# Graph stack, layer 2: the maximum of the squared norms travels over the partitions by two DMAs through memory

## The chip, the cores and the metric

One Trainium2 chip, one core of it. The metric is device time in microseconds (us) of one execution; three runs of the kernel before are given, and their median counts. The engines are called PE (TensorE), DVE (VectorE), ACT (ScalarE), POOL (GpSimd) and SP (SyncE, which here only issues DMAs).

## What is computed

Four graph layers in a row on x of 16 graphs x 1024 nodes x 64 features, with one adjacency matrix of 1024 x 1024. Each layer takes `h = max(layernorm(x), 0)` and adds its result to x. Layers 0 and 3 are graph attention with additive scores, layer 1 is an attention by channel, layer 2 is the one of this change:

```
def _gat_layer(h, mask, b):
    scores = einsum('...nd,...md->...nm', h, h)
    scores = where(mask, scores, NEG)
    attn = softmax(scores, axis=-1)
    return einsum('...nm,...md->...nd', attn, h) + b

h = einsum('bnc,hdc->bhnd', x, Wh)                 # 4 heads of 64
out_h = _gat_layer(h, mask, bh)
z = leaky_relu(concatenated heads, 0.2)
h2 = einsum('bnk,dk->bnd', z, Wo)
out2 = _gat_layer(h2, mask, bo)                    # the output attention
out = layernorm(leaky_relu(out2, 0.2)) * gamma + beta
```

The softmax needs an upper bound of the scores so that the exponential stays finite. A score is a dot product of two rows of h, so no score is above the largest squared norm of a row. That maximum over the 1024 nodes is what the change is about.

## The kernel before, in words

Layer 2 is a list of 80 **units** (`UNITS`): for each of 16 graphs the heads 0 and 1, then the output attention of the graph before, then heads 2 and 3; the last unit (`LAST`) is the output attention of the last graph and runs inside layer 3. Nodes lie on 128 partitions in 8 tiles, so a unit has 8 **weights** (jt = 0 to 7). For each weight PE makes scores of 128 x 1024 into one of two PSUM tiles (`dots`, L1795), ACT takes the exponential into a ring in SBUF (`weights`, L1042), DVE multiplies by the mask (`masked_weights`, L1388), and PE multiplies it with the values and sums (`dot_sums`, `weigh`, L1614). PE runs its sums three weights behind its scores (`LAG`).

Every engine's order is written out by hand. Beside the weights of unit n the kernel prepares unit n+1 (`nxt`), at fixed weights of each engine's `dot_unit`:

- PE: values (jt 0, `values`, L1838) and their transposes (jt 2, `features`, L1847) into a PSUM pair `AX`, whose two banks have their users in an order that `AX_AT` lists; a user waits until the one before has given the bank back (`ax_free`). Twice in a graph it also turns finished heads (`turn_heads`, L1815), which takes both banks: at jt 5 of head 3 and at jt 6 of the next graph's head 0.
- ACT: copies the values and squares them (`sq`, L1063), copies the transposes as fp16 (`hi`, L1076).
- DVE: row sums of the squares and their maximum per partition (`norms`, jt 1: L1413, `norm2_max` L1415); the fp16 remainder of the transposes (`feature_rest`, jt 3: `lo`, L1405), which gives bank 1 back; the end of the unit before (`epilogue`, jt 3: `recip` L1396, `leaky` L1397, shown as score); the bound (`bias`, jt 4: `norm2_all` L1421, `dot_bias` L1423). Buffer digits are left out in the profile, so `norm2_max` reads norm_max.
- PE, for the bound: `spread_bound` (jt 3) multiplies the column `norm2_max`, broadcast, with the identity, so that every partition gets all 128 maxima as a row in bank 0 of `AX` (`spread`, L1604, the line is shared with the two attention layers). DVE's `bias` reads that row and gives bank 0 back.
- SP: for each unit four DMAs move `hi` into `FA`, and when `lo` is made four more move `lo` (L507, L508, L513, L514). The first `dots` of the next unit wait until all eight have landed. Each wait holds back every later DMA of SP.

ACT's first exponential of a unit waits for its `dot_bias`; POOL divides a finished unit (`divide`, L794) after DVE's epilogue.

Of the kernel before, what the change touches and what calls it, by code (L numbers as in the profile page):

```python
# [11 lines left out]
P = 128  # L12
D = 64
ALU = mybir.AluOpType
ACT = mybir.ActivationFunctionType
F32 = mybir.dt.float32
# [14 lines left out]
def gnn_stack(nc, x, adj, w_gat0, w_gat0_t, a_gat0, w0, b0, wa, ba, wh_t, bh, wo_t, bo, gamma, beta,  # L31
# [11 lines left out]
    with ExitStack() as ctx:  # L43
# [85 lines left out]
        norm2_max = sb("norm2_max", [P, 1])  # L129
        norm2_all = sb("norm2_all", [P, 1])  # L130
        dot_bias = sb("dot_bias", [P, 3])

# [140 lines left out]
        sq_made = sem("sq_made")  # L273
        bound_dve = sem("bound_dve")
        z_epi = sem("z_epi")
        on_dve = sem("on_dve")
# [130 lines left out]

        def place_bound(u):

            place(("N", u["n"]), 0)  # L410

        def place_pair(name, b, q):
# [7 lines left out]
        place_features(UNITS[0])  # L420
        place_bound(UNITS[0])
        for u in UNITS[:-1]:
            if after(u):
                place_values(after(u))
                place_features(after(u))
                place_bound(after(u))
            if is_head(u, 0) and u["b"] > 0:
                place_pair("Z", u["b"] - 1, 2)
            if is_head(u, 2) and u["b"] + 1 < B:
                place_norm(2, u["b"] + 1)  # L430
            if u is BEFORE:
                place_norm(3, 0)
                place_peak(3, 0)
                place_norm(3, 1)
            if is_head(u, 3):
                place_pair("Z", u["b"], 0)
# [10 lines left out]
        place_features(LAST)  # L447
        place_bound(LAST)
        place_peak(3, FIRST + 1)
# [39 lines left out]
        def _(sp):  # L489
# [10 lines left out]
            for u in UNITS:  # L500
                par = buf_of(u)
                moved = features_in[par]
                sp.wait_ge(hi_made, u["n"] + 1)
                for half in range(2):
                    cols_of = slice(half * HALF, (half + 1) * HALF)
                    own = slice(half * D, (half + 1) * D)
                    sp.dma_start(FA[0:D, par, 0, cols_of], hi[own, par, :]).then_inc(moved, 16)  # L507
                    sp.dma_start(FA[D:P, par, 1, cols_of], hi[own, par, :]).then_inc(moved, 16)  # L508
                sp.wait_ge(lo_made, u["n"] + 1)
                for half in range(2):  # L510
                    cols_of = slice(half * HALF, (half + 1) * HALF)
                    own = slice(half * D, (half + 1) * D)
                    sp.dma_start(FA[D:P, par, 0, cols_of], lo[own, par, :]).then_inc(moved, 16)  # L513
                    sp.dma_start(FA[0:D, par, 1, cols_of], lo[own, par, :]).then_inc(moved, 16)  # L514
# [642 lines left out]
        def _(dve):  # L1157
# [259 lines left out]
            def bias(u):  # L1417
                buf = buf_of(u)
                k, at = AX_AT["N", u["n"]]
                dve.wait_ge(ax_full[k], at + 1)  # L1420
                dve.tensor_reduce(norm2_all[:, :], AX[k][:, 0:P], AX_X, ALU.max).then_inc(ax_free[k], 1)  # L1421
                dve.wait_ge(ax_free[k], at + 1)
                dve.tensor_scalar(dot_bias[:, buf:buf + 1], norm2_all[:, :], -1.0, DOT_LIFT, ALU.mult, ALU.add)\  # L1423
                    .then_inc(bound_dve, 1)
# [18 lines left out]
            def dot_unit(u, jt):  # L1443
# [3 lines left out]
                if jt == 1 and nxt:  # L1447
                    norms(nxt)
                if jt == 3 and nxt:
                    feature_rest(nxt)  # L1450
                if jt == 3 and 0 < u["n"] < LAST["n"]:
                    epilogue(UNITS[u["n"] - 1])
                if jt == 4 and nxt:
                    bias(nxt)
# [28 lines left out]
            def last_layer():  # L1483
# [13 lines left out]
                for jt in range(T):  # L1497
                    gat_weights(3, 1, jt)
                    if jt == 0:
                        node_peak(3, 2)  # L1500
                        stat_mean(3, B - 2)
                    if jt == 2:
                        gat_reciprocal(3, 0)
                    if jt == 3:
                        norms(LAST)
                    if jt == 5:
                        feature_rest(LAST)
                    if jt == 6:
                        bias(LAST)
                    if jt == 7:  # L1510
                        stat_var(3, B - 2)

                for jt in range(T):
# [40 lines left out]
        def _(pe):  # L1554
# [159 lines left out]
            def last_layer():  # L1714
# [12 lines left out]
                for jt in range(T):  # L1727
# [5 lines left out]
                    if jt == 2:  # L1733
                        features(LAST)
                    if jt == 4:
                        spread_bound(LAST)

# [111 lines left out]

            def spread_bound(u):  # L1850

                pe.wait_ge(bound_dve, 3 * u["n"] + 2)
                spread(take_bank(AX_AT["N", u["n"]]), norm2_max[:, 0:1])

            def turn_next(b):
                turn_norm(2, b)

            def dot_unit(u, jt):
# [3 lines left out]
                if jt == LAG - 1 and after(u):  # L1862
                    features(after(u))
                if jt == 3 and after(u):
                    spread_bound(after(u))
                if jt == 6 and is_head(u, 0) and b > 0:
# [12 lines left out]
            def dot_layer():  # L1879
                spread_bound(UNITS[0])  # L1880
                end = T * LAST["n"]
# [56 lines left out]
```

## Time and profile before

| | us |
|---|---|
| median of 3 runs (2016.5 to 2019.79) | 2018.07 |
| span of the profiled execution, first to last instruction | 2015.0 |
| PE busy in the span | 1913.5 (95%) |
| DVE busy | 1684.4 (84%) |
| ACT busy | 1234.0 (61%) |
| POOL busy | 1065.5 (53%) |

The profiled execution's own time is its span with what lies around it. The page gives the span; against the lowest of the runs 1.5 us lie around it, against the median 3.1 us. TensorE's granted clock is 0.987 of full speed over the span. Layer 2 takes the time from about 440 us to about 1780 us.

### The profile page before, as it was taken

Reading aid. Unit: us, or ns where it says so; the run is one execution under the profiler, and the core shown is the slowest. Engines: PE = TensorE matmul, PEld = TensorE weight load, DVE = VectorE, ACT = ScalarE, POOL = GpSimd, SP = SyncE. Lnnn points to the kernel's source line nnn. Section 1 sums busy time; section 2 is a strip of 40 time slices with the busy share of each in tenths; the row PEclk is TensorE's granted clock in tenths of the full one; section 3 lists DMA queues with packets and bytes.
Section 4 is the critical chain, followed back from the end, with each engine's and each line's share of the span. In section 5 each row is a group of like instructions: output and inputs, shape, how many; then the busy total and the mean of one; then the engine's idle time right before and its main releaser. Section 6 shows DMA issues by size and latency. Waiting matters only on the chain.

```text
span 2015.0 us, 95064 instructions
## 1 busy us (share of the span) xinstructions
PE 1913.5 (95%) x43624; PEld 1569.7 (78%) x43624; DVE 1684.4 (84%) x2007; ACT 1234.0 (61%) x1842; POOL 1065.5 (53%) x754
## 2 busy tenths in 40 slices
PE   7888789989999999999999999999999999989998
PEld 6777689977777777777777777777777777767887
DVE  6988988868788888888888888888888888867998
ACT  5776655426666666666666666666666666654342
POOL 6787888622344545545454544545545445354653
PEclk8999999989999999999999999999999999999999
DMA  7000000001111111111111111111111111101111
GB/s 181 4 4 3 3 2 2 2 14 38 32 33 34 33 34 34 35 34 35 34 35 34 33 34 34 29 36 30 33 34 35 34 35 34 34 14 24 25 25 35
DMA packets 88255, 61.24 MB, mean 30 GB/s; under 512 B 45616, under 2 KB 86832, under 8 KB 87856
## 3 DMA queue, kind: packets, MB, share of 16 engines
q1 hardware_dynamic: 85632, 54.57, 11.1%
q8 instruction: 343, 5.62, 1.2%
q10 hardware_dynamic: 2224, 0.59, 0.1%
q14 instruction: 56, 0.46, 0.1%
HBM read 8.98 MB, written 4.19 MB: 7 GB/s over the span
## 4 chain that ended last, share of the span: by engine, by line
PE 70%; DVE 13%; POOL 9%; ACT 4%; issue 3%; DMA 0%; SPq 0%; ACTq 0%; POOLq 0%; DVEq 0%
PE ACC L1614 30%; PE S L1795 24%; PE S L1774 5%; DVE ring L1388 4%; PE AX L1838 3%; PE AX L1847 2%; DVE ring L1241 2%; PE AX L1815 2%; POOL sp_log L778 1%; POOL ln_sq L781 1%; DVE ch_rden L1373 1%; POOL below L626 1%; PE AX L1594 1%; POOL st_rstd L553 1%; ACT ring L1042 1%
## 5 line engine op out<-in xcount | busy, mean ns | idle before, releaser
L1614 PEld LDWEIGHTS ACC<-V,ring 128*64 128x64 f32 x28672 | 957.4, 138 | 184.6 <-issue 38.8
L1388 DVE TENSOR_TENSOR ring<-ring,mask_self_t 128x1024 f32<-128x1024 f32 x640 | 893.2, 1405 | 192.3 <-ACT ring L1042 187.9
L1614 PE MATMUL ACC<-V,ring 128*64 128x65 f32 x28672 | 976.7, 223 | 31.7 <-DVE ring L1241 13.7
L1042 ACT ACTIVATE ring<-S,dot_bias 128x1024 f32<-128x1024 f32 x640 | 713.8, 1116 | 410.3 <-PE S L1795 373.1
L1795 PE MATMUL S<-FA 128*64 128x512 f16 x5120 | 666.1, 382 | 1.4 <-DMA FA<-lo 1.4
L1795 PEld LDWEIGHTS S<-FA 128*64 128x64 f16 x5120 | 253.5, 110 | 161.1 <-ACT ring L1042 15.8
L1241 DVE SCALAR_TENSOR_TENSOR ring<-S,pair_q,mask_t 128x1024 f32<-128x1024 f32 x256 | 315.1, 1272 | 15.3 <-DVE f_max L1253 4.7
L794 POOL TENSOR_TENSOR EV_both<-score,recip 128x512 f32<-128x512 f32 x64 | 124.4, 1943 | 316.5 <-DVE score L1397 316.4
L1774 PE MATMUL S<-parts,mask_t 128*128 128x128 bf16 x3072 | 176.0, 220 | 12.9 <-DVE X L1377 11.6
L1774 PEld LDWEIGHTS S<-parts,mask_t 128*128 128x128 bf16 x3072 | 174.3, 99 | 14.6 <-issue 14.6
L787 POOL TENSOR_TENSOR V<-v_pairs,bh_bc 128x512 f32<-128x512 f32 x64 | 96.6, 1509 | 119.2 <-ACT v_pairs L1062 119.2
L866 ACT ACTIVATE accs<-ACC 128x520 f32<-128x520 f32 x112 | 66.8, 597 | 90.3 <-PE ACC L1614 90.3
L593 POOL TENSOR_TENSOR ln_rstd<-ln_ve,neg_half 128x8 f32<-128x8 f32 x32 | 74.0, 2311 | 79.2 <-DVE ln_ve L1232 66.8
L794 POOL TENSOR_TENSOR relu_z<-score,recip 128x512 f32<-128x512 f32 x16 | 30.4, 1900 | 108.8 <-DVE score L1397 108.8
L1062 ACT ACTIVATE v_pairs<-AX 128x512 f32<-128x512 f32 x80 | 47.8, 598 | 56.1 <-PE AX L1838 56.1
L553 POOL TENSOR_TENSOR st_rstd<-st_ve,neg_half 128x8 f32<-128x8 f32 (+1 forms) x31 | 66.1, 2133 | 22.3 <-ACT st_ve L899 17.5
L642 POOL TENSOR_TENSOR V<-V 128x512 f32<-128x512 f32 x32 | 33.3, 1041 | 56.7 <-ACT V L923 56.6
L778 POOL TENSOR_TENSOR sp_log<-relu_z,on_mean 128x512 f32<-128x512 f32 x16 | 30.4, 1901 | 54.2 <-DVE on_mean L1431 54.2
L1413 DVE TENSOR_REDUCE norm<-sq 128x8 f32<-128x512 f32 x80 | 54.1, 677 | 5.2 <-ACT sq L1063 5.2
L1373 DVE RECIPROCAL ch_rden<-S 128x512 f32<-128x512 f32 x16 | 53.6, 3348 | 5.7 <-PE S L1774 5.4
L1405 DVE TENSOR_TENSOR lo<-AX,hi 128x512 f16<-128x512 f32 x80 | 54.6, 682 | 1.1 <-ACT hi L1076 1.1
L1847 PE MATMUL AX<-ident,v_pairs 128*128 128x128 f32 x320 | 53.3, 290 | 1.5 <-ACTq L1068 1.5
(131 smaller groups left out, 2017.6 us busy)
## 6 DMA issues: line engine op xcount, KB each, us to landing
FA<-hi SPq DMA_DIRECT2D x320, 64.0 KB, 2.0
FA<-lo SPq DMA_DIRECT2D x320, 64.0 KB, 2.0
X<-in_x SPq DMA_DIRECT2D x16, 256.0 KB, 5.0
ring<-in_adj SPq DMA_DIRECT2D x8, 512.0 KB, 8.1
out_x<-X SPq DMA_DIRECT2D x16, 256.0 KB, 2.6
wh<-in_wh_t ACTq DMA_DIRECT2D x2, 64.0 KB, 6.5
bh_bc<-in_bh ACTq DMA_DIRECT2D x1, 128.0 KB, 9.5
w_gat<-in_w_gat ACTq DMA_DIRECT2D x4, 16.0 KB, 3.9
```

What stands on the lines that cost most here:

```text
L553: pool.tensor_tensor(stat_of(st_rstd, layer, b, count), stat_of(st_ve, layer, b, count), neg_half[:, 0:count * T], ALU.pow).then_inc(st_rs ...
L593: pool.tensor_tensor(ln_rstd[:, :], ln_ve[:, :], neg_half[:, 0:T], ALU.pow).then_inc(ln_pool, 1)
L787: pool.tensor_tensor(halves_of(V[:, u["n"] % 3, :, 1:D + 1]), v_pairs, halves_of(chans(bias)), ALU.add)\
L794: pool.tensor_tensor(dst, tiles(leaky[:, :]), cols(recip[:, :]), ALU.mult).then_inc(z_epi, 1)
L1042: act.activation(ring[:, jt, :], S[jt % 2][:, :], ACT.Exp, bias=dot_bias[:, n % 2:n % 2 + 1])\
L1241: dve.scalar_tensor_tensor(out=ring[:, jt, :], in0=S[par][:, :], scalar=pair_q[:, par, jt:jt + 1], in1=mask_t[:, jt, :], op0=ALU.max, op1= ...
L1373: dve.reciprocal(tiles(ch_rden[:, :]), sums[:, :, D:2 * D]).then_inc(ch_recip, 1)
L1388: dve.tensor_tensor(ring[:, jt, :], ring[:, jt, :], mask_self_t[:, jt, :], ALU.mult)\
L1614: last = pe.matmul(acc_of(t)[rows, :], ring[:, jt, t * P + c * CUT:t * P + (c + 1) * CUT], values, start=(jt == 0 and t % 4 == 0), stop=(j ...
L1774: last = pe.matmul(S[par][:, t * P:(t + 1) * P], mask_t[:, j, t * P:(t + 1) * P], parts[:, par, part, j, :], start=(j == 0 and part == 0), ...
L1795: last = pe.matmul(S[jt % 2][rows, cut], FA[:, buf, 0, jt * P + c * CUT:jt * P + (c + 1) * CUT], FA[:, buf, i, cut], start=(i == 0), stop= ...
L1847: last = pe.transpose(AX[k][:, q * P:(q + 1) * P], v_by_pair[:, q * P:(q + 1) * P], ident[:, :])
```

## The change

`norm2_max`, one number per partition, is written by a DMA to a row of 128 floats in memory, and a second DMA reads that row back into every partition (`norm2_bc`, 128 x 128). SP issues the first ahead of the four `hi` moves, the second between `hi` and `lo`. DVE's `bias` reads `norm2_bc` instead of PSUM, at jt 6 instead of 4 (for the last unit after jt 7 of its unit of layer 3 instead of after 6). The epilogue of the unit before goes to jt 2 instead of 3, ahead of the third weight's `lo`. PE's `spread_bound` and its place among the users of bank 0 are gone. In the changed file the lines after the declarations lie a few numbers further (L1388 is L1390, L1795 is L1793).

```diff
+        norm2_row = nc.dram_tensor("norm2_row", [2, P], F32, kind="Internal").ap()
+        norm2_bc = sb("norm2_bc", [P, P])
...
-        def place_bound(u):
-            place(("N", u["n"]), 0)
...
@@ SP
             for u in UNITS:
                 par = buf_of(u)
                 moved = features_in[par]
+                sp.wait_ge(bound_dve, 3 * u["n"] + 2)
+                sp.dma_start(norm2_row[par], norm2_max[:, 0:1]).then_inc(bound_out, 16)
                 sp.wait_ge(hi_made, u["n"] + 1)
                 for half in range(2):
...
+                sp.wait_ge(bound_out, 16 * (u["n"] + 1))
+                sp.dma_start(norm2_bc[:, :], norm2_row[par].partition_broadcast(P)).then_inc(bound_in, 16)
                 sp.wait_ge(lo_made, u["n"] + 1)
@@ DVE
             def bias(u):
                 buf = buf_of(u)
-                k, at = AX_AT["N", u["n"]]
-                dve.wait_ge(ax_full[k], at + 1)
-                dve.tensor_reduce(norm2_all[:, :], AX[k][:, 0:P], AX_X, ALU.max).then_inc(ax_free[k], 1)
-                dve.wait_ge(ax_free[k], at + 1)
+                dve.wait_ge(bound_in, 16 * (u["n"] + 1))
+                dve.tensor_reduce(norm2_all[:, :], norm2_bc[:, :], AX_X, ALU.max).then_inc(bound_maxed, 1)
+                dve.wait_ge(bound_maxed, u["n"] + 1)
                 dve.tensor_scalar(dot_bias[:, buf:buf + 1], norm2_all[:, :], -1.0, DOT_LIFT, ALU.mult, ALU.add)\
                     .then_inc(bound_dve, 1)
...
+                if jt == 2 and 0 < u["n"] < LAST["n"]:
+                    epilogue(UNITS[u["n"] - 1])
                 if jt == 3 and nxt:
                     feature_rest(nxt)
-                if jt == 3 and 0 < u["n"] < LAST["n"]:
-                    epilogue(UNITS[u["n"] - 1])
-                if jt == 4 and nxt:
+                if jt == 6 and nxt:
                     bias(nxt)
...
-                    if jt == 6:
-                        bias(LAST)
                     if jt == 7:
                         stat_var(3, B - 2)
+                        bias(LAST)
@@ PE
-            def spread_bound(u):
-                pe.wait_ge(bound_dve, 3 * u["n"] + 2)
-                spread(take_bank(AX_AT["N", u["n"]]), norm2_max[:, 0:1])
...
-                if jt == 3 and after(u):
-                    spread_bound(after(u))
```

PE in head 3 of a graph, before, from the transposes of the next unit to the turning of heads 0 and 1 (EV_both is where finished heads lie):

```order
L1847 MATMUL AX<-ident,v_pairs 128x128 x4
L1795 MATMUL S<-FA 64x512 x8
L1614 MATMUL ACC<-V,ring 64x65 x16
L1604 MATMUL AX<-ident,norm_max 64x128 x2
L1795 MATMUL S<-FA 64x512 x8
L1614 MATMUL ACC<-V,ring 64x65 x16
L1795 MATMUL S<-FA 64x512 x8
L1614 MATMUL ACC<-V,ring 64x65 x16
L1815 MATMUL AX<-ident,EV_both 128x128 x8
```

PE at the same place, now:

```order
L1845 MATMUL AX<-ident,v_pairs 128x128 x4
L1793 MATMUL S<-FA 64x512 x8
L1614 MATMUL ACC<-V,ring 64x65 x16
L1793 MATMUL S<-FA 64x512 x8
L1614 MATMUL ACC<-V,ring 64x65 x16
L1793 MATMUL S<-FA 64x512 x8
L1614 MATMUL ACC<-V,ring 64x65 x16
L1813 MATMUL AX<-ident,EV_both 128x128 x8
```

The two matmuls of the spread are gone, and with them a user of bank 0 between the values and the turned heads.

DVE in the same head 3, before, from the norms to the bound, with each row's waits:

```order
L1413 TENSOR_REDUCE norm<-sq 128x8 [waits sq_made]
L1415 TENSOR_REDUCE norm_max<-norm 128x1 [waits bound_dve]
L1388 TENSOR_TENSOR ring<-ring,mask_self_t 128x1024 [waits exp_done] x2
L1405 TENSOR_TENSOR lo<-AX,hi 128x512 [waits hi_made]
L1396 RECIPROCAL recip<-accs 128x8 [waits lo_made,acc_copied]
L1397 SCALAR_TENSOR_TENSOR score<-accs 128x512
L1388 TENSOR_TENSOR ring<-ring,mask_self_t 128x1024 [waits exp_done]
L1421 TENSOR_REDUCE norm_all<-AX 128x1 [waits ax_full0]
L1423 TENSOR_SCALAR dot_bias<-norm_all 128x1 [waits ax_free0]
```

DVE at the same place, now:

```order
L1415 TENSOR_REDUCE norm<-sq 128x8 [waits sq_made]
L1417 TENSOR_REDUCE norm_max<-norm 128x1 [waits bound_dve]
L1390 TENSOR_TENSOR ring<-ring,mask_self_t 128x1024 [waits exp_done]
L1398 RECIPROCAL recip<-accs 128x8 [waits acc_copied]
L1399 SCALAR_TENSOR_TENSOR score<-accs 128x512
L1390 TENSOR_TENSOR ring<-ring,mask_self_t 128x1024 [waits exp_done]
L1407 TENSOR_TENSOR lo<-AX,hi 128x512 [waits hi_made]
L1390 TENSOR_TENSOR ring<-ring,mask_self_t 128x1024 [waits lo_made,exp_done]
L1390 TENSOR_TENSOR ring<-ring,mask_self_t 128x1024 [waits exp_done] x2
L1422 TENSOR_REDUCE norm_all<-norm_bc 128x1 [waits bound_in]
L1424 TENSOR_SCALAR dot_bias<-norm_all 128x1 [waits bound_maxed]
```

The epilogue stands one weight sooner and now ahead of `lo`; the bound stands two weights later and waits for a DMA.

SP, the DMAs of one unit, now (before, there are the four of `hi` and the four of `lo` alone):

```order
L502 DMA norm_row<-norm_max 128x1 [waits bound_dve]
L507 DMA FA<-hi 64x512 [waits hi_made]
L508 DMA FA<-hi 64x512
L510 DMA norm_bc<-norm_row 128x128 [waits bound_out]
L515 DMA FA<-lo 64x512 [waits lo_made]
L516 DMA FA<-lo 64x512
```

The rows of `hi` and of `lo` each stand there twice, one pair after the other. One DMA is added ahead of `hi`, and one, with a wait for the first, ahead of `lo`.

## Rows read from the trace of the kernel before

**Rows 1.** The page, busy time and the chain that ended last, by engine.

```profile
PE 1913.5 (95%) x43624; PEld 1569.7 (78%) x43624; DVE 1684.4 (84%) x2007; ACT 1234.0 (61%) x1842; POOL 1065.5 (53%) x754
...
PE 70%; DVE 13%; POOL 9%; ACT 4%; issue 3%; DMA 0%; SPq 0%; ACTq 0%; POOLq 0%; DVEq 0%
```

**Rows 2.** Busy time by stretch: 15 graphs of layer 2, with clock and DMA share.

```profile
480.00:1760.00 1280.00, 1260.35 (x27648) 994.00 (x27646) 1078.90 (x1303) 856.93 (x972) 602.71 (x331) 1.00 0.14 34
```

**Rows 3.** Waits of PE: total us, times, longest us.

```profile
PE AX L1815 <- DVE norm_all L1421: 19.6, 15, 1.7
...
PE S L1795 <- DMA FA<-lo: 1.4, 1, 1.4
```

**Rows 4.** The chain in order of time, 1014 to 1044 us: start, us, what.

```profile
1016.10 0.61 DVE lo L1405
...
1016.85 0.20 DVE recip L1396
1017.05 0.56 DVE score L1397
...
1018.75 0.21 DVE norm_all L1421
...
1019.09 1.07 PE AX L1815 x8
...
1032.50 0.22 PE AX L1604 x4
1032.72 0.86 PE S L1795 x8
```

**Rows 5.** The tile norm_max: duration min/median/max in ns of each operation.

```profile
L1604 PE MATMUL AX<-ident,norm_max x320: 272/274/323, 439.1 to 1830.8; 128*64 128x128 f32 x160
```

**Rows 6.** The tile FA: issue of one DMA in ns, and all landings.

```profile
L508 SPq DMA_DIRECT2D FA<-hi x160: 593/597/1960, 428.7 to 1831.2; - x160
...
DMA to landing us min/median/max: 1.9/2.0/3.6
```

**Rows 7.** The tile out_x, the only one that DMAs write to memory.

```profile
DMA to landing us min/median/max: 2.5/2.6/4.2
```

**Rows 8.** DMA issues, KB each and median us to landing: the smallest elements.

```profile
a_gat<-in_a_gat ACTq DMA_DIRECT2D x2, 0.5 KB, 5.3
```

**Rows 9.** Timeline of SP: last `lo` issue of four units; last of `hi` in one.

```profile
455.93 0.60 SPq L514 DMA_DIRECT2D FA<-lo  x1
...
1153.20 0.60 SPq L508 DMA_DIRECT2D FA<-hi  x1
...
1157.22 0.60 SPq L514 DMA_DIRECT2D FA<-lo  x1
...
1189.97 0.60 SPq L514 DMA_DIRECT2D FA<-lo  x1
...
1774.26 0.60 SPq L514 DMA_DIRECT2D FA<-lo  x1
```

**Rows 10.** Timeline of PE: first scores of the four units that follow those moves.

```profile
459.21 1.03 PE L1795 MATMUL S<-FA 128*64 128x512 f16 x8
...
1159.86 1.03 PE L1795 MATMUL S<-FA 128*64 128x512 f16 x8
...
1195.17 1.03 PE L1795 MATMUL S<-FA 128*64 128x512 f16 x8
...
1776.59 1.03 PE L1795 MATMUL S<-FA 128*64 128x512 f16 x8
```

**Rows 11.** Timeline of DVE in one output unit, 1148 to 1162 us; idle time in brackets.

```profile
1150.95 0.16 DVE L1415 TENSOR_REDUCE norm_max<-norm 128x1 f32<-128x8 f32 x1
...
1152.94 1.34 DVE L1388 TENSOR_TENSOR ring<-ring,mask_self_t 128x1024 f32<-128x1024 f32 x1 [0.63 <-ACT ring L1042]
1154.21 0.68 DVE L1405 TENSOR_TENSOR lo<-AX,hi 128x512 f16<-128x512 f32 x1
...
1157.41 4.15 DVE L1388 TENSOR_TENSOR ring<-ring,mask_self_t 128x1024 f32<-128x1024 f32 x3
```

More of the change, by code:

```diff
@@ L274, in gnn_stack @@
         bound_dve = sem("bound_dve")
+        bound_out = sem("bound_out")
+        bound_in = sem("bound_in")
+        bound_maxed = sem("bound_maxed")
         z_epi = sem("z_epi")
@@ L420, in gnn_stack @@
         place_features(UNITS[0])
-        place_bound(UNITS[0])
         for u in UNITS[:-1]:
@@ L425, in gnn_stack @@
                 place_features(after(u))
-                place_bound(after(u))
             if is_head(u, 0) and u["b"] > 0:
@@ L447, in gnn_stack @@
         place_features(LAST)
-        place_bound(LAST)
         place_peak(3, FIRST + 1)
@@ L1734, in last_layer @@
                         features(LAST)
-                    if jt == 4:
-                        spread_bound(LAST)
                 for jt in range(T + LAG):
@@ L1879, in dot_layer @@
             def dot_layer():
-                spread_bound(UNITS[0])
                 end = T * LAST["n"]
```

## The prediction

> **What bounds the kernel now.** Read the busy time first [rows 1]: PE is busy for 95% of the span, and 70% of the chain that ended last is PE's. Then take layer 2 by itself. Over 15 graphs, 1280.00 us, PE is busy for 1260.35 us at a granted clock of 1.00, the upper of its two levels (2.4 GHz) [rows 2]. So PE idles for 19.65 us there, and the list of PE's waits says where: 19.6 us, 15 times, always at the turning of finished heads (L1815), always for DVE's maximum L1421 [rows 3]. Nothing else makes PE wait in this stretch. What is taken off PE here shortens the kernel one for one, until something else is late. DVE is busy for 1078.90 of the 1280.00 us [rows 2] and has room.
>
> The chain in order of time shows one of the 15 waits [rows 4]: DVE ends `lo` at 1016.71, does the epilogue (0.20 and 0.56), one mask, the maximum until 1018.96, and only then PE turns heads, because the maximum holds bank 0. Later in the same rows the spread takes 0.22 us of PE, and the scores behind it take their usual 0.86.
>
> **What is removed.** The spread has 320 matmul records, four per unit, so 80 units [rows 5]; one alone lasts 274 ns, but they overlap, and its step on the chain is 0.22 us [rows 4]. The first unit's lies before layer 2 has PE busy, the last one's in layer 3, so I count 78 x 0.22 = 17.2 us. The wait of 19.6 us goes as well: bank 0 is then last used by the next unit's values, which ACT copies out several weights earlier, and the heads being turned were finished two units before. Together **36.8 us**. DVE's maximum and its follower remain, about 0.4 us a unit; read from SBUF instead of PSUM I price them as before.
>
> **What is late next in head 3.** The turning also needs bank 1, which `lo` gives back. PE would be ready at 1019.09 less 19.6 / 15 = 1.31, less 0.22, so at about 1017.55, and at bank 1 half of its 1.07 later, 1018.1. `lo` ended at 1016.71 [rows 4]. It is now behind the epilogue (0.8 with the gaps), and in head 2 the bound now stands ahead of the output's mean, on which POOL and then this DVE sequence wait: 0.4 more. That is 1017.9, and some 0.1 to release the bank. So between nothing and 0.3 us is left of each wait; I take 0.1 x 15 = **1.5 us** given back.
>
> **The epilogue sooner.** In four of five units DVE idles before the mask of weight 3, 0.63 us in the unit shown [rows 11], so the epilogue fills that hole and `lo` comes only about 0.15 later; in head 0, which has hardly a hole, I take 0.6 to 1.0, in head 3 1.2 as above. The sums that the epilogue reads have been copied by ACT more than 1 us before, and POOL's division, off the path, starts sooner.
>
> **The bound later.** In the unit of rows 11 the masks of weights 5 to 7 run from 1157.41 to 1161.56, so that of weight 6 ends near 1160.3. The bound (0.4) leaves the place ahead of them and comes back behind weight 6: ready near 1160.3. ACT needs it when the next unit's first scores are done, 1159.86 + 0.86 - 0.22 = 1160.5 [rows 4, 10]. Were it later, PE would notice only at the unit's third score tile, two steps of 0.86 + 0.93 on. I cost it at nothing.
>
> **The DMAs: the term that decides.** PE starts a unit when the last `lo` has landed. All landings of `FA` take 1.9 to 3.6 us, median 2.0, and one issue on SP takes 0.6, up to 1.96 [rows 6]. With 2.0, the four moves shown leave 1.3, 0.6, 3.2 and 0.3 us before PE's first scores [rows 9, 10]; in one unit PE did wait [rows 3]. This margin now loses 0.22 in every unit, 1.31 more in head 3, the delay of `lo`, and whatever SP's queue adds.
>
> SP first waits for the norms' maximum, ready at 1151.11 in the unit shown [rows 11]; the write's issue takes up to 0.6, so the four `hi` issues end about 0.3 later than the 1153.80 seen [rows 9], at 1154.1. Then SP waits for the write. No DMA of the trace writes so little to memory. Bounds: 1.9 as the fastest `FA` move [rows 6], 5.3 as the smallest elements at the crowded start [rows 8]. I take 2.6, the median of the only writes to memory [rows 7]: landed at about 1153.75, before SP is done with `hi`. The broadcast's issue ends at 1154.7, and `lo` is ready at about 1155.05, so SP holds nothing back.
>
> The Trainium skill ("DMA: Bandwidth & Descriptors", section "Anatomy of one DMA") puts a DMA's fixed cost at about 2.0 us, mostly the receipt from the memory written to, which agrees with the 2.0 of rows 6. The same page ("Specifications") says that below 512 B the engine reads, modifies and writes. Were that a second round trip, the write would land after 4.0 us (an estimate from that page), and the sum would give back some 10 us more.
>
> I made the same subtraction for each of the 78 units from its own rows of these two views (rows 9 and 10 hold the first and the last of them): 15 come up short, by 8.3 us in all, mostly where an issue had taken over 1 us. The broadcast is 64 KB and stands just ahead of `lo` in the same queue; if `lo` lands 0.3 later for it, the shortfall is 14.7. I take the middle, **12 us** given back. For the last unit the broadcast's issue (0.6) falls on a landing that PE waited for already [rows 3]: **0.6 us**.
>
> **Sum.** -36.8 + 1.5 + 12 + 0.6 = -22.7 us. The profiled span is 2015.0, and 3.1 us below the median of 2018.07 with what lies around it; on the span the sum gives 1992.3, on the median 1995.4. I say **1995 us**.
>
> **Rivals.**
> *The broadcast holds `lo` up* by about one issue spacing (0.64 us between starts [rows 9]). For it: five kinds of unit have margins of that size. Against it: it is issued before `lo` is ready, in the pause. The same subtraction then gives 29 us, with the other terms a sum of -6: 2012. At 0.8 the shortfall is 37 and the gain is gone. Chance 0.18, of it 0.08 faster, 0.07 same, 0.03 slower.
>
> *The write lands late and SP stands in front of `lo`*: the mechanism for slower. Every later DMA of SP waits for it, so each unit's `lo` is late together. Below about 3.3 us it costs nothing; at 4.2, the slowest write to memory [rows 7], 24 us; from about 4.5 (37 us) the change loses; at 5.3 [rows 8] 88 us, with the other terms 2071. Against it: the queue is quiet here (DMA share 0.14 [rows 2]), and the 5.3 was seen beside loads of megabytes. Chance 0.11.
>
> *The wait in head 3 only changes its bank*: `lo` releases bank 1 some 0.6 us later than I reckon, and 15 x 0.6 = 9 us come back: 2004. Chance 0.07, still faster.
>
> **How the numbers follow.** 0.2% of the time, 4 us, is what a measurement of this kernel can tell from no change. The forecast has 0.64. Faster: 0.64 + 0.08 + 0.07 = 0.79; same 0.07; slower 0.03 + 0.11 = 0.14. Range: nothing given back is 2018.1 - 36.8 = 1981; the upper end takes in the first rival at one issue spacing, 2013. Above it lie the late write and the rest of that rival, together 0.2.
>
> **What would show it.** Right: no spread records; PE's list of waits without L1421 (at most some us on `lo` at the turning); instead waits of the first scores of a unit on the DMA of `lo`, some 12 us over about 20 units; the write landing within 3 us and the broadcast's issue right behind the fourth `hi`; PE busy in layer 2 still near 98%. Wrong: SP's queue waiting on the write in most units, `lo` issues starting over 0.5 us after `lo` is made, ACT's exponentials waiting for the bound, or DVE's masks becoming what PE's sums wait for.

## The result and the profile after

The changed kernel takes 2498.98 us (median of 4 runs, 2497.85 to 2506.09) against 2018.2: 1.239 times as long, interval [1.2374, 1.2409]. The forecast was 1995 us, faster than before; the measured time is 24% longer, far beyond the range. Its profiled execution took 2506.09 us, its span 2504.2.

The page of the changed kernel, busy time and the two lines of the chain that ended last (by engine, by line):

```profile
PE 2061.1 (82%) x43304; PEld 1664.4 (66%) x43304; DVE 1637.8 (65%) x2007; ACT 1233.3 (49%) x1842; POOL 998.9 (40%) x754
...
DMA 31%; PE 30%; DVE 10%; SPq 9%; ACT 8%; issue 6%; POOL 5%; ACTq 0%; POOLq 0%; DVEq 0%
DMA norm_row<-norm_max 21%; PE ACC L1614 12%; DMA FA<-lo 9%; PE S L1793 8%; SPq L515 4%; PE S L1772 4%; PE AX L1836 4%; DVE ring L1390 4%; ACT ring L1044 3%; SPq L516 3%; DVE norm L1415 2%; DVE ring L1243 2%; ACT v_pairs L1064 1%; ACT sq L1065 1%; SPq L510 1%
```

Where the chain was PE's for 70% [rows 1], its largest single item is now the write of 128 numbers, 512 bytes in all: 21% of the span. Who waits because of it stands in the lists of waits, of PE first, then of SP and of DVE (total us, times, longest us):

```profile
PE S L1793 <- DMA FA<-lo: 304.4, 77, 6.9
PE ACC L1614 <- issue: 62.7, 41, 4.3
PE S L1793 <- issue: 13.3, 13, 2.6
```

```profile
SPq L510 <- DMA norm_row<-norm_max: 293.1, 69, 6.2
```

```profile
DVE norm_all L1422 <- DMA norm_bc<-norm_row: 240.1, 76, 6.4
```

The turning of the heads is gone from PE's list, as forecast [rows 3]. But PE now waits 304.4 us for `lo` at the start of nearly every unit, and 76 us where the profile shows no releaser ("issue").

One unit on SP's timeline shows the order of events:

```profile
1315.36 0.33 SPq L502 DMA_DIRECT2D norm_row<-norm_max  x1
...
1317.51 0.60 SPq L508 DMA_DIRECT2D FA<-hi  x1
1322.93 0.33 SPq L510 DMA_DIRECT2D norm_bc<-norm_row  x1
1323.30 0.46 SPq L515 DMA_DIRECT2D FA<-lo  x1
...
1325.08 0.60 SPq L516 DMA_DIRECT2D FA<-lo  x1
```

The write is issued at 1315.36 and SP goes on only at 1322.93, 7.6 us later. Over the 80 units this distance is 7.38 to 10.18 us, median 8.07; the forecast had 2.6 for the landing. `lo` was made at 1319.03 and is issued at 1323.30. (The write counts as acknowledged, or landed, when its semaphore has received all 16 increments; here the last one came at 1322.91.)

The stretches of that pause, by engine (us, PE, PEld, DVE, ACT and POOL busy, clock, DMA share, GB/s), and PE's timeline in it:

```profile
1315.00:1320.00 5.00, 5.00 (x110) 3.85 (x112) 4.76 (x8) 2.88 (x4) 2.11 (x1) 1.00 0.26 56
1320.00:1322.90 2.90, 0.47 (x17) 0.33 (x11) 0.41 (x1) 0.00 (x0) 0.00 (x0) 1.00 0.00 0
1322.90:1328.00 5.10, 4.54 (x85) 3.42 (x85) 2.45 (x2) 3.83 (x4) 0.00 (x0) 1.00 0.16 54
```

```profile
1319.38 1.10 PE L1614 MATMUL ACC<-V,ring 128*64 128x65 f32 x31
1322.94 0.24 PE L1614 MATMUL ACC<-V,ring 128*64 128x65 f32 x1 [2.47 <-issue]
```

From about 1320.5 to 1322.9 no compute engine works. The DMA share reads 0.00 because it counts a packet in the stretch in which it starts; the trace's packet records do have one under way, 16 KB on the queue that brings instructions, from 1319.52 to 1322.31. PE stops before the last of 32 matmul records of one sum, a place where its program waits for nothing, and goes on when the write is acknowledged. So it is not only SP's wait that hurts.

The third loss is the clock. Over the 15 graphs of layer 2:

```profile
480.00:2250.00 1770.00, 1423.31 (x27754) 1100.84 (x27750) 1045.56 (x1319) 869.03 (x986) 545.42 (x335) 0.90 0.11 28
```

About as many matmuls as in [rows 2] keep PE busy for 1423 instead of 1260 us, at a granted clock of 0.90 instead of 1.00: after the pauses it falls to the lower of its two levels (1.2 GHz) for a while. For the whole program PE's busy time rises by 2061.1 - 1913.5 = 148 us, though the spreads (17) are gone. With 303 more for `lo` (304.4 less 1.4), 69 more without a releaser (62.7 + 13.3 = 76.0, less 6.6 before) and 19.6 saved, that makes 500 us; the spans of the two profiled executions differ by 489.

### The profile page after: what moved, and what is told of

It is laid out like the page before. It is cut to its first block, busy times and chain, and to the rows that moved or that the text cites. A ratio compares the mean times of both kernels' runs of the same rounds, so it can differ in the third digit from the quotient of the medians.

```text
span 2504.2 us, 94504 instructions
## 1 busy us (share of the span) xinstructions
PE 2061.1 (82%) x43304; PEld 1664.4 (66%) x43304; DVE 1637.8 (65%) x2007; ACT 1233.3 (49%) x1842; POOL 998.9 (40%) x754
## 4 chain that ended last, share of the span: by engine, by line
DMA 31%; PE 30%; DVE 10%; SPq 9%; ACT 8%; issue 6%; POOL 5%; ACTq 0%; POOLq 0%; DVEq 0%
DMA norm_row<-norm_max 21%; PE ACC L1614 12%; DMA FA<-lo 9%; PE S L1793 8%; SPq L515 4%; PE S L1772 4%; PE AX L1836 4%; DVE ring L1390 4%; ACT ring L1044 3%; SPq L516 3%; DVE norm L1415 2%; DVE ring L1243 2%; ACT v_pairs L1064 1%; ACT sq L1065 1%; SPq L510 1%
## 5 line engine op out<-in xcount | busy, mean ns | idle before, releaser
L1614 PEld LDWEIGHTS ACC<-V,ring 128*64 128x64 f32 x28672 | 1026.2, 145 | 246.1 <-issue 115.2
L1390 DVE TENSOR_TENSOR ring<-ring,mask_self_t 128x1024 f32<-128x1024 f32 x640 | 835.7, 1311 | 510.2 <-ACT ring L1044 483.8
L1614 PE MATMUL ACC<-V,ring 128*64 128x65 f32 x28672 | 1046.4, 230 | 81.6 <-issue 62.7
L1793 PE MATMUL S<-FA 128*64 128x512 f16 x5120 | 734.3, 410 | 319.3 <-DMA FA<-lo 304.4
L1793 PEld LDWEIGHTS S<-FA 128*64 128x64 f16 x5120 | 267.2, 116 | 518.0 <-DMA FA<-lo 315.2
L789 POOL TENSOR_TENSOR V<-v_pairs,bh_bc 128x512 f32<-128x512 f32 x64 | 86.5, 1352 | 407.2 <-ACT v_pairs L1064 407.1
L796 POOL TENSOR_TENSOR EV_both<-score,recip 128x512 f32<-128x512 f32 x64 | 103.7, 1621 | 266.2 <-DVE score L1399 266.1
L1422 DVE TENSOR_REDUCE norm_all<-norm_bc 128x1 f32<-128x128 f32 x80 | 22.9, 286 | 240.1 <-DMA norm_bc<-norm_row 240.1
L586 POOL TENSOR_TENSOR ln_xc<-X,ln_mean 128x512 f32<-128x512 f32 x16 | 21.5, 1344 | 175.0 <-DVE ln_mean L1227 175.0
L1836 PE MATMUL AX<-wh,h_t 64*64 64x64 f32 x2048 | 60.7, 279 | 0.8 <-ACTq L865 0.8
```

Of the source, the lines that this page charges most:

```text
L789: pool.tensor_tensor(halves_of(V[:, u["n"] % 3, :, 1:D + 1]), v_pairs, halves_of(chans(bias)), ALU.add)\
L796: pool.tensor_tensor(dst, tiles(leaky[:, :]), cols(recip[:, :]), ALU.mult).then_inc(z_epi, 1)
L1390: dve.tensor_tensor(ring[:, jt, :], ring[:, jt, :], mask_self_t[:, jt, :], ALU.mult)\
L1614: last = pe.matmul(acc_of(t)[rows, :], ring[:, jt, t * P + c * CUT:t * P + (c + 1) * CUT], values, start=(jt == 0 and t % 4 == 0), stop=(j ...
L1793: last = pe.matmul(S[jt % 2][rows, cut], FA[:, buf, 0, jt * P + c * CUT:jt * P + (c + 1) * CUT], FA[:, buf, i, cut], start=(i == 0), stop= ...
L1836: last = pe.matmul(AX[half][c * CUT:(c + 1) * CUT, t * D:(t + 1) * D], rows, w, start=(i == 0), stop=(i == chunks[-1]), skip_group_check=True)
```

## The experiments

Two theories. **R (receipt):** the write itself is acknowledged late, and until then the DMA rings hold up what stands behind it: the moves' completions, and PE's instructions. **Q (queue order):** only SP's wait in front of `lo` costs.

### The read behind lo

```diff
-                sp.wait_ge(bound_out, 16 * (u["n"] + 1))
-                sp.dma_start(norm2_bc[:, :], norm2_row[par].partition_broadcast(P)).then_inc(bound_in, 16)
                 sp.wait_ge(lo_made, u["n"] + 1)
...
                     sp.dma_start(FA[0:D, par, 1, cols_of], lo[own, par, :]).then_inc(moved, 16)
+                sp.wait_ge(bound_out, 16 * (u["n"] + 1))
+                sp.dma_start(norm2_bc[:, :], norm2_row[par].partition_broadcast(P)).then_inc(bound_in, 16)
```

> The changed kernel, with SP's wait for the write and the broadcast read moved behind the four moves of lo. Theory R (receipt): the write of 128 four-byte elements to memory is acknowledged only 7.4 to 10.2 us after its issue, and until then the DMA rings deliver no completion of the moves behind it and no instructions either. Then lo is issued at once but still lands no sooner than about 9 us after the norms' maximum (12 in the changed kernel), PE keeps the stalls without a releaser (76 us in the changed kernel), and the bound comes some 13 us after the maximum, so ACT waits for it: 2150 to 2300 us. Theory Q (queue order): only SP's wait in front of lo costs, the slow write holds up nothing else. Then PE's waits for lo (304 us in the changed kernel) fall to some 20, the stalls without a releaser go, and only the late bound is left, about 1 us a unit: 2000 to 2090 us.

Measured: 2214.56 us, 1.098 of before [1.0955, 1.0999]. PE's waits, then ACT's:

```profile
PE S L1793 <- DMA FA<-lo: 122.3, 61, 4.6
PE ACC L1614 <- issue: 29.4, 31, 3.5
```

```profile
ACT ring L1044 <- DVE dot_bias L1424: 243.4, 70, 15.4
```

The time lies in R's range: SP's place in the queue is worth 284 us, but with `lo` issued at once PE still waits 122 us for it, and the bound is now late for ACT. The stops without a releaser fell to 29.4 us, though, where R had them stay at 76, and not all of the 122 us is the slow write's: the run with the row in SBUF further down has the same order on SP and a quick write, and there PE still waits 63 us for `lo` and ACT 229 us for the bound. The two runs differ by 90 us.

### The write alone

The kernel before, with SP's wait for the maximum and the write ahead of `hi`; the matmul spread stays, and nothing reads the row.

```diff
+                sp.wait_ge(bound_dve, 3 * u["n"] + 2)
+                sp.dma_start(norm2_row[par], norm2_max[:, 0:1]).then_inc(bound_out, 16)
                 sp.wait_ge(hi_made, u["n"] + 1)
```

> The kernel before, with nothing but the write of the column of maxima to memory added in SP's queue ahead of hi; nothing waits for it before the end, and its result is not used (the bound comes from the matmuls as before). Theory R: the completions of hi and lo are held until the write is acknowledged, about 8 us after its issue, where lo landed 7.7 to 8.0 us after the maximum before; PE's waits for lo rise from 1.4 to 30 to 100 us and PE shows stalls without a releaser of 50 to 100 us: 2080 to 2250 us. Theory Q: a write that nobody waits for costs its issue on SP, 0.3 us a unit off the path: 2016 to 2030 us.

Measured: 2125.42 us, 1.054 [1.0514, 1.0556]. PE's waits and, from the two pages, the queue that brings instructions, here and before (packets, MB, share of 16 engines' span):

```profile
PE S L1800 <- DMA FA<-lo: 42.1, 39, 2.6
PE ACC L1619 <- issue: 36.7, 33, 3.1
```

```profile
q8 instruction: 343, 5.62, 1.5%
```

```profile
q8 instruction: 343, 5.62, 1.2%
```

Nobody waits for this write, and it costs 107 us. Q falls. The same 343 instruction packets occupy the engines for 1.5% of a longer span instead of 1.2%. The packet records of the traces say it more sharply. From 450 us on to 230 us before the end, the packets of 16 KB on this queue took at most 1.6 us each in the kernel before (227 of them). With the unused write they took up to 3.5 us, and 70 of 226 more than 2 us; in the changed kernel up to 3.9 us, and 85 of 224 more than 2 us. That PE's stops without a releaser are a lack of instructions is the reading that fits; no row ties a stop to a packet.

### What makes the write slow

Five more writes at the same place in the kernel before, unused as well; only the write's shape differs. Here are the arguments of the DMA, shortened, against those of the write alone:

```diff
-norm2_row[par]                              # "norm2_row", [2, P]
+norm2_row[par, :, 0:1]                      # "norm2_row", [2, P, P]: 512 bytes apart (write_pitch512)
+norm2_row[par, :, 0:1]                      # [2, P, 16]: 64 bytes apart; [2, P, 4]: 16 bytes apart
+norm2_row[par, 0:16], norm2_max[0:16, 0:1]  # 16 elements side by side (write_16)
+norm2_row[par], norm2_wide[:, :]            # [2, P, P]: 512 whole bytes of each partition (write_512B)
```

> The kernel before with the unused write of the 128 maxima to memory, but each four-byte element 512 bytes from the next instead of side by side. Theory P (the 128 partial writes meet in one 512-byte row and are done one after the other): apart from each other they run side by side, acknowledged within 4 us, no stalls without a releaser beyond the 7 us of before: 2016 to 2040 us. Theory F (any four-byte write to memory is slow by itself): as with the elements side by side, 2110 to 2140 us.

> The kernel before with an unused write of a 128 x 128 tile (64 KB, 512 bytes from each partition) to memory at the same place of SP's queue. If the cause is the partial write, whole 512-byte rows are acknowledged like the writes of the output (2.6 us) and only the 64 KB in the queue cost: 2016 to 2045 us. If any write to memory in front of the moves holds their completions: 2080 to 2150 us.

> The kernel before with the unused write of the first 16 maxima alone (one element for each of 16 DMA engines). If the delay grows with the number of elements in the row (about 45 ns each over a base of 2 us: 128 take 7.7), the write is acknowledged in under 3 us and costs nothing: 2014 to 2030 us. If it is a fixed delay of a partial write: 2080 to 2140 us.

> The kernel before with the unused write of the 128 maxima to memory, the four-byte elements 64 bytes apart (eight in each 512 bytes). If what makes partial writes wait for each other is a piece of memory of 512 bytes or more, as the side-by-side run and the 512-byte run leave open: 2030 to 2130 us and an acknowledgement of 3 to 8 us. If it is 64 bytes or less: 1.4 us and 2014 to 2024 us, as with 512 bytes.

> The kernel before with the unused write, elements 16 bytes apart in the order of the partitions, so that four neighbours share 64 bytes. Theory S: of an engine's eight elements four and four share a piece, so about half the delay of side by side: acknowledged in 3 to 5 us, 2018 to 2070 us. Rival (it is the whole dense 512-byte row): like 64 bytes apart, 1.4 us, 2014 to 2024 us.

| write | us | ratio to before | issue to landing, median us |
|---|---|---|---|
| 128 elements side by side | 2125.42 | [1.0514, 1.0556] | 7.1 (see below) |
| 512 bytes apart | 2019.23 | [0.9989, 1.0013] | 1.4 |
| 64 bytes apart | 2018.51 | [0.9985, 1.001] | 1.4 |
| 16 bytes apart | 2024.48 | [1.0021, 1.0048] | 1.5 |
| 16 elements side by side | 2029.21 | [1.003, 1.0071] | 1.3 |
| 512 whole bytes each | 2020.64 | [0.9993, 1.0014] | 1.5 |

The tile's landings (min/median/max) at 64 bytes and at 16 bytes apart:

```profile
DMA to landing us min/median/max: 1.4/1.4/3.5
```

```profile
DMA to landing us min/median/max: 1.4/1.5/3.5
```

The page of the write alone gives no landing, because its trace has only 854 of the 1280 semaphore increments; the last one recorded of each write came a median 7.1 us after the issue, the first 2.9. At 512 bytes apart all 16 increments of a write came between 1.2 and 1.4 us.

So neither a write to memory nor the four-byte element is slow. Slow are many four-byte elements packed together: 128 in one run of 512 bytes, while 16 in a run of 64 bytes land after 1.3 us. The Trainium skill ("DMA: Bandwidth & Descriptors", "Specifications") has a read-modify-write below 512 B; every row of the table but the last lies below, and those with some distance take no longer than whole rows.

A quick landing is not the whole price. 16 elements side by side and 128 at 16 bytes apart cost 10 and 6 us, small but outside the noise (the first from two runs, and expected to cost nothing). PE waits 12.6 and 8.3 us for `lo` there, and 17 and 12 of the instruction packets take more than 2 us. At 64 bytes apart PE waits 1.7 us and no packet takes that long.

### The same bytes in another order

If one DMA engine's eight neighbouring elements wait for each other, a permuted row would cure it; the maximum does not see the order.

```diff
-                sp.dma_start(norm2_row[par], norm2_max[:, 0:1]).then_inc(bound_out, 16)
+                sp.dma_start(norm2_row[par].rearrange("(i e) -> e i", i=8), norm2_max[:, 0:1], allow_slow_non_contiguous=True).then_inc(bound_out, 16)
```

> The changed kernel with one thing else: the 128 maxima go to the same 512 bytes of memory in another order (eight neighbouring partitions land 64 bytes apart, and every 64 bytes hold one element of each sixteenth of the partitions), which the maximum over them does not see. Theory S (a DMA engine's eight elements fall into one or two 64-byte pieces side by side, and each partial write waits for the one before it in its piece, about 0.8 us each): in the new order no engine writes a piece twice, the write is acknowledged in about 1.4 us, and the forecast's sum holds at last, with the 6.7 us that a read from memory cost by itself and the 8 us of the sooner epilogue in place of my 12: 1988 to 2003 us. Rival P (the 128 partial writes wait for each other anywhere in one 512-byte row, whichever engine sends them): 2400 to 2520 us as in the changed kernel.

> The kernel before with the unused write in that order. Theory S: acknowledged in about 1.4 us, 2014 to 2025 us. Rival P: 6 to 8 us and 2110 to 2140 us, as with the elements in the order of the partitions.

> The run permuted_row with the epilogue back at weight 3, behind lo. By itself the sooner epilogue cost 6 to 10 us, put down to lo coming later: if the same holds here, 3 to 10 us less than permuted_row. Rival: with bank 0 free the sooner epilogue no longer stands on the path, and the two agree within 3 us.

Measured: 2364.49 us for the changed kernel with this row [1.1675, 1.1745], 2099.73 for the write alone [1.0355, 1.0455], 2372.84 with the epilogue back [1.1732, 1.1814]. SP still waits for the write:

```profile
SPq L510 <- DMA norm_row<-norm_max: 237.7, 71, 4.6
```

Theory S falls: the write alone still lands after 7.3 us (median of the last increments recorded), and most of the loss stays. It goes with the dense run as such, whichever engine writes where. Rival P's ranges were missed as well, by 36 and 10 us: the order is worth 134 us in the changed kernel, and why stays open. The last of the three told nothing about the epilogue, since the slow write covers it.

### The row in SBUF

```diff
-        norm2_row = nc.dram_tensor("norm2_row", [2, P], F32, kind="Internal").ap()
+        norm2_row = sb("norm2_row", [1, 2, P])
...
-                sp.dma_start(norm2_row[par], norm2_max[:, 0:1]).then_inc(bound_out, 16)
+                sp.dma_start(norm2_row[0:1, par, :], norm2_max[:, 0:1]).then_inc(bound_out, 16)
...
-                sp.dma_start(norm2_bc[:, :], norm2_row[par].partition_broadcast(P)).then_inc(bound_in, 16)
+                sp.dma_start(norm2_bc[:, :], norm2_row[0:1, par, :].unsqueeze(1).broadcast_to([1, P, P])).then_inc(bound_in, 16)
```

> The changed kernel, with the row of 128 maxima in SBUF (one partition) instead of memory; the same 128 four-byte elements, the same order on every engine. Theory R (the memory's receipt of 128 partial writes to one 512-byte row): the first DMA lands in about 2 us like the moves within SBUF, the broadcast too, and the forecast's sum holds: 1985 to 2015 us. Rival E (the four-byte elements are slow wherever they go): the wait of SP stays at 7 to 8 us and the time at 2400 to 2550 us.

Measured: 2035.54 us, 1.009 [1.0076, 1.0109]. DMA issues (KB, median us to landing):

```profile
FA<-lo SPq DMA_DIRECT2D x320, 64.0 KB, 3.0
norm_bc<-norm_row SPq DMA_DIRECT2D x80, 64.0 KB, 4.2
...
norm_row<-norm_max SPq DMA_DIRECT2D x80, 0.5 KB, 1.9
```

The first DMA is as quick as R said, and 463 of the 481 us are gone. But the time lies above R's 2015 us, and the forecast's gain is not there: the broadcast from one partition takes 4.2 us, `lo` behind it lands after 3.0 instead of 2.0 [rows 6], and PE waits 44.3 us for it.

With that broadcast moved behind `lo`:

> The run with the row in SBUF, with the broadcast moved behind the four moves of lo on SP. There lo landed a median 2.66 us after its last issue (2.0 before) and PE waited 44 us for it, which I put down to the broadcast ahead of it in the queue, whose 128 reads come from one partition (3.9 us to landing). If so, lo lands after 2.0 again, PE's waits for lo fall under 15 us, and the forecast's gain shows: 1983 to 2000 us. Rival: the bound, now some 10 us after the maximum, holds up ACT's first exponential of each unit and then PE: 2000 to 2035 us, with ACT or DVE waiting for the broadcast in most units.

Measured: 2124.15 us, 1.052 [1.0499, 1.0534]. The rival had the mechanism, but the loss is some 90 us beyond its range. DVE stands in front of the broadcast, with its masks behind it, and PE waits more:

```profile
DVE norm_all L1422 <- DMA norm_bc<-norm_row: 201.9, 79, 5.3
```

```profile
PE S L1793 <- DMA FA<-lo: 63.0, 44, 3.0
PE AX L1813 <- DVEq L1409: 23.5, 14, 1.9
```

`lo` does land after 2.0 us again, as expected, but PE's waits for it rise from 44 to 63 us instead of falling under 15. So the broadcast ahead of `lo` is not the only thing that makes `lo` late for PE. L1409 is where DVE gives bank 1 back after `lo`.

### The terms of the forecast one by one

The read from memory alone, a row of the adjacency matrix, unused, between `hi` and `lo` of the kernel before (later units wait for the one before, which has long landed):

```diff
+                wait(sp, bound_out, 16 * u["n"])
+                sp.dma_start(norm2_bc[:, :], adj[0, 0:P].partition_broadcast(P)).then_inc(bound_out, 16)
                 sp.wait_ge(lo_made, u["n"] + 1)
```

> The kernel before with nothing but a broadcast read of 512 bytes of memory (a row of the adjacency matrix, unused) to all partitions, in SP's queue between hi and lo. The forecast took 4 us for such a read in front of lo, at a landing near 2.6 us; the row in SBUF showed a median of 0.66 us more for lo and 44 us of PE's waits. If the read from memory holds lo up as that one did: PE waits 30 to 50 us for lo, 2040 to 2070 us. If it stays as forecast: 2018 to 2030 us.

Measured: 2025.31 us, 1.003 [1.0018, 1.0041], landing after 3.2 us. This is within the forecast's range: 6.7 us more, with `lo` landing after 2.4 us instead of 2.0 and PE waiting 9.6 us for it.

The epilogue alone:

```diff
+                if jt == 2 and 0 < u["n"] < LAST["n"]:
+                    epilogue(UNITS[u["n"] - 1])
                 if jt == 3 and nxt:
                     feature_rest(nxt)
-                if jt == 3 and 0 < u["n"] < LAST["n"]:
-                    epilogue(UNITS[u["n"] - 1])
```

> The kernel before with the epilogue at weight 2 instead of 3 and nothing else. The forecast held that lo then comes 0.15 to 0.8 us later inside its margin and that nothing else on the path moves: 2014 to 2024 us, the 15 waits at the turning unchanged. Rival: lo is late in enough units, and PE waits for it by 20 us or more: 2030 to 2045 us.

Measured: 2026.46 us, 1.0035 [1.0019, 1.0051], a miss of 2 us: a small loss, between the two.

```profile
PE AX L1815 <- DVE norm_all L1421: 22.8, 14, 1.8
...
PE S L1795 <- DMA FA<-lo: 7.6, 10, 1.7
```

PE waits 6 us more for `lo` and 3 more at the turning, together about the loss of 7.8 us.

The wait at the turning, removed without any DMA:

```diff
-                if jt == 5 and is_head(u, 3):
+                if jt == 6 and is_head(u, 3):
                     turn_heads(b, 0)
```

> The kernel before, with heads 0 and 1 turned one weight later in head 3 (jt 6 instead of 5), so that DVE's maximum has left bank 0 by then. If the 19.6 us of PE's waits there are on the path, as the forecast held: 1995 to 2002 us, and L1421 leaves PE's list of waits. Rival: the output unit's values then wait for the turned heads, or another engine is as late: 2012 to 2022 us.

Measured: 1997.42 us, 0.9899 [0.9884, 0.9914]: 20.8 us less, the forecast's 19.6 in full. PE's busy time of layer 2 now fills its stretch:

```profile
480.00:1740.00 1260.00, 1258.55 (x27626) 992.95 (x27622) 1056.99 (x1302) 859.81 (x971) 606.52 (x332) 1.00 0.14 34
```

And with the spread in bf16:

```diff
-        norm2_max = sb("norm2_max", [P, 1])
+        norm2_max = sb("norm2_max", [P, 1], BF16)
...
-                    last = pe.matmul(AX[k][c * CUT:(c + 1) * CUT, 0:P], column.broadcast_to([P, CUT]), ident[:, :],
+                    last = pe.matmul(AX[k][c * CUT:(c + 1) * CUT, 0:P], column.broadcast_to([P, CUT]), unit[:, :],
...
-                spread(take_bank(AX_AT["N", u["n"]]), norm2_max[:, 0:1])
+                spread(take_bank(AX_AT["N", u["n"]]), norm2_max[:, 0:1], ident_bf)
```

> The run with the heads turned later (1997.4 us), and the spread in bf16 instead of fp32: the column of maxima is written as bf16 and multiplied with the bf16 identity (the bound of the scores is then rounded, by at most 0.4%, which the softmax takes out again). A spread in fp32 costs PE 0.22 us on the path in each of 78 units; with half the matmul passes or fewer it should cost 0.06 to 0.11: 9 to 12 us less, 1985 to 1990 us. Rival: PE's time at that place is not bound by the passes, or the margin of lo is eaten: 1994 to 2000 us.

Measured: **1990.03 us**, 0.9852 [0.9836, 0.9868], the fastest of all runs. Its chain shows the spread at a quarter [rows 4], and PE's list a new small wait:

```profile
1038.55 0.06 PE AX L1604 x2
```

```profile
PE AX L1815 <- POOL EV_both L794: 3.3, 13, 0.5
```

The spread should give 78 x 0.16 = 12.5 us; 7.4 came, a little under the 9 to 12 expected. PE's new wait for POOL's division at the turning takes back 3.3, and its waits for `lo` rise from 1.9 to 5.4.

### The change with rows apart

Everything of the change, but the row in eight pieces of 16 elements, 512 bytes apart:

```diff
-        norm2_row = nc.dram_tensor("norm2_row", [2, P], F32, kind="Internal").ap()
+        norm2_row = nc.dram_tensor("norm2_row", [2, 8, P], F32, kind="Internal").ap()
...
+                sp.dma_start(norm2_row[par, :, 0:16].rearrange("i e -> e i"), norm2_max[:, 0:1], allow_slow_non_contiguous=True).then_inc(bound_out, 16)
...
+                sp.dma_start(norm2_bc[:, :].rearrange("p (i e) -> p i e", i=8), norm2_row[par, :, 0:16].partition_broadcast(P)).then_inc(bound_in, 16)
```

> The changed kernel, with the 128 maxima spread over eight rows of memory 512 bytes apart, 16 side by side in each (each DMA engine writes one element to every row), and the broadcast reading those eight pieces of 64 bytes. Theory P (partial writes to one 512-byte piece are done one after another, some 55 ns each: 16 and 32 per piece were acknowledged in 1.3 to 1.6 us, 128 in 7 to 8): acknowledged in under 2 us, SP no longer waits for it, and the forecast's sum holds with the read's 6.7 us and the epilogue's 8 us in place of my 12: 1988 to 2005 us. Rival: the broadcast of 1024 pieces of 64 bytes stands in front of lo as the row in SBUF did: 2020 to 2050 us, PE waiting 30 us or more for lo.

> The run rows_apart with the epilogue back at weight 3, behind lo. If the sooner epilogue costs by delaying lo (8 us when alone in the kernel before): 4 to 10 us less than rows_apart. If it pays here, because the turning of the heads waits for POOL's division otherwise, or DVE's order is better filled: 0 to 10 us more.

Measured: 2035.32 us, 1.0105 [1.0087, 1.0123]; with the epilogue back 2040.64, 1.0123 [1.0106, 1.014]. PE's longest wait, and the landings of `FA`:

```profile
PE S L1793 <- DMA FA<-lo: 44.1, 40, 2.9
```

```profile
DMA to landing us min/median/max: 1.9/2.4/4.8
```

The write now lands in a median of 2.3 us, a little over the 2 expected, and SP no longer waits for it. 464 of the 481 us are back. What is left fits the first rival of the forecast, larger than I had it; no run took this wait away by itself. Putting the epilogue back changes nothing that the intervals can tell; here SP's own queue, not `lo`, sets the issue in most units.

## Why the prediction was wrong

*What bounds the kernel, and what is removed: right.* The 19.6 us at the turning are real and came back in full when only that was moved (20.8 us). The spread's 0.22 us is on the path: cut to 0.06, it gave 7.4 of 12.5 us. Bank 1 did not become the new wait in the changed kernel; neither it nor the run with rows apart has a wait of the turning for `lo`. The third rival did come in the two runs in which the late bound held DVE up: PE waits for bank 1 at the turning for 20.0 us with the read behind `lo`, and for 23.5 us with the row in SBUF read late.

*The step that failed: "I take 2.6, the median of the only writes to memory".* The write lands after 7 to 8 us, outside both bounds (1.9 and 5.3). The rows it was taken from write 256 KB in whole rows, and the nearest in size were reads. None writes many small elements side by side, and that is what costs. Nor was 5.3 the landing of the smallest elements. In the same list of the kernel before stand two reads of 128 four-byte elements each, behind other loads:

```profile
w_c<-in_w ACTq DMA_DIRECT2D x1, 0.5 KB, 10.8
b_c<-in_b ACTq DMA_DIRECT2D x1, 0.5 KB, 11.4
```

The rival of the late write had the right mechanism for the larger half. Continued from its 88 us at 5.3 to the measured 8.07, in 78 units, it gives 88 + 78 x 2.77 = 304 us of waits for `lo`, and PE waited 304.4. That the two agree so closely is luck, since a part of these waits does not come from SP's place in the queue (42 us remain where nobody waits for the write). The rival's chance and price were cut off by the bound of 5.3. The fixed 2.0 us that the prediction quotes from the Trainium skill ("DMA: Bandwidth & Descriptors", "Anatomy of one DMA") is stated there for DMAs that GpSimd issues; by themselves, SP's writes of small elements to memory landed here after 1.3 to 1.5 us or after 7 to 8, and the 4.0 us estimated from it was far too low for the dense one.

*What no step had.* A write in the queue delays others than the one that waits for it. Alone and unwaited for, it costs 107 us: PE waits 42 us for moves that SP issued on time, stops for 37 us in the middle of its sums, and its granted clock falls from 0.987 to 0.979 over the span.

*The landing of lo, 12 us.* Mis-sized as well: with a quick write PE still waits 44 us for `lo`, and the kernel takes 2035 us, outside the range even so. The read alone cost 6.7 us and the epilogue alone 7.8. By themselves the 512-byte-apart write, the read and the epilogue add 4, 8 and 6 us to PE's waits for `lo`; together, with PE faster by the spread and the turning, they add 43. The reading that fits is that the margin is one and the same: the write's issue, the broadcast's issue and transfer, the later `lo` and the faster PE all draw on it. My subtraction took the queue's delays from median rows and let the broadcast wait in a pause that was no longer there: with rows apart SP waits for `lo` in 15 units, before in 66. PE's busy time in that run is 1914.0 us, against 1913.5 with the spreads still in it, so their 17 us came back. By the granted clock of the two spans, 0.982 against 0.987, some 10 of these are clock (an estimate, 2037.5 x 0.018 - 2015.0 x 0.013); the rest stays open. -36.8 + 43 + 17 is 23 against a measured 19.

*The bound later, at nothing.* Right only while the broadcast lands early. In the changed kernel DVE waits 240 us for it, from the same slow write; with the row in SBUF and the broadcast behind `lo`, where the write is quick, DVE waits 202 us for it and ACT 229 us for the bound, in a kernel of 2124 us.

## What to carry to other kernels

A DMA's price depends on how its elements lie in memory, so a landing time must come from a row with the same layout: a column of 128 floats written into 512 dense bytes took 7 to 8 us, and 1.4 us with 64 bytes between them. When DMAs feed the engine that bounds a kernel, look for the margin before the last landing first; here it was 0.3 to 3.2 us in the units shown, and three additions that cost little one by one used it up together. An engine's wait of 1.3 us once in five units was cheaper to remove by moving its own work one step than by taking another road.

## What the runs showed of the hardware beyond that

- 128 four-byte writes packed into 512 bytes of memory are acknowledged 7 to 8 us after issue, in either order tried; 16 side by side, or 128 with 16, 64 or 512 bytes from one to the next, in 1.3 to 1.5. A fixed time for each write, one after another, does not fit: at the 55 ns that 128 in 7 us would give, the 32 that share 512 bytes at 16 bytes apart would take 1.8 us on top of the rest, and they landed after 1.5 in all. Why the dense run is slow stays open.
- While such a write is outstanding, packets that bring 16 KB of instructions take up to 3.5 to 3.9 us instead of at most 1.6, moves that were issued on time keep PE waiting (42 us in the write alone), and PE stops where its program waits for nothing (1320.5 to 1322.9 us above).
- One broadcast of 512 bytes to all partitions takes 4.2 us from a single partition of SBUF and 3.2 us from memory; in both cases the moves of `lo` queued right behind it land later (3.0 and 2.4 us instead of 2.0).
